# A decoder layer on one core: row sums of attention added on GpSimd, and the value products moved among the thirds of Q and K

## The reference, cut to what matters

```
qkv = x @ w_attn + b_attn ;  q, k, v = split(qkv), 16 heads of 32
att = softmax(where(causal, (q @ k.T) / sqrt(32), -inf))
y   = att @ v                      # per head
x   = layernorm(x + y @ w_proj + b_proj)
x   = layernorm(x + chosen(x))     # one of 4 experts by token id
x   = layernorm(x + routed(x))     # top 2 of 8 experts and a shared one
```

## Time and profile before

| what | value |
|---|---|
| median of 3 runs | 1278.62 us (1278.06 to 1281.37) |
| profiled execution, its own time | 1269.57 us |
| its span | 1267.7 us |
| mean granted PE clock | 0.968 |
| busy, share of span: PE, weight load, DVE, ACT, POOL | 93%, 74%, 54%, 36%, 19% |
| attention stage, roughly | 0 to 450 us of the span |

### The profile page before, as it was taken

How to read it: one execution, slowest core, us unless ns; L and a number is a source line. 1 busy time by engine, 2 the same in 40 slices (tenths; PEclk the granted TensorE clock), 3 DMA queues, 4 the chain that set the end, 5 groups by cost and what they waited for, 6 DMA issues and landing times.

```text
span 1267.7 us, 20196 instructions
## 1 busy us (share of the span) xinstructions
PE 1183.1 (93%) x6404; PEld 935.7 (74%) x6404; DVE 686.9 (54%) x1469; ACT 456.2 (36%) x699; POOL 240.8 (19%) x370
## 2 busy tenths in 40 slices
PE   7788999999999879994999999999999999999996
PEld 5565676576575558883688888899999997778885
DVE  5564656656557546664447634343444442666744
ACT  3254435334435322222343334244444433333331
POOL 2021314413414410003100440000000000433200
PEclk8989999999999979997999999999999999999998
DMA  7336573532524222225223666245345531666440
GB/s 241 86 100 238 179 249 118 133 88 51 150 61 125 80 85 83 84 76 157 101 82 93 208 227 199 79 149 175 122 145 172 171 99 53 206 178 195 144 139 33
DMA packets 129277, 169.72 MB, mean 134 GB/s; under 512 B 17553, under 2 KB 70801, under 8 KB 129169
## 3 DMA queue, kind: packets, MB, share of 16 engines
q1 hardware_dynamic: 115360, 136.64, 35.2%
q0 software_dynamic: 8496, 28.32, 6.7%
q10 hardware_dynamic: 5312, 3.42, 1.2%
HBM read 95.98 MB, written 47.19 MB: 113 GB/s over the span
## 4 chain that ended last, share of the span: by engine, by line
PE 74%; DVE 8%; SPq 5%; POOL 3%; DMA 3%; issue 3%; ACT 2%; ACTq 1%; POOLq 0%; DVEq 0%
PE routed_ps L819 18%; PE routed_ps L1370 16%; PE psT L471 11%; SPq L354 5%; PE chosen_psG L819 4%; PE chosen_psY L819 4%; PE routed_ps L1389 2%; PE routed_ps L1390 2%; PE routed_ps L1391 2%; PE psS L537 2%; PE psO L576 2%; POOL routed_rows_io L1308 2%; PE psN L576 2%; PE psE L558 2%; PE routed_ps L1411 1%
## 5 line engine op out<-in xcount | busy, mean ns | idle before, releaser
L471 PE MATMUL psT<-store 128*128 128x512 f32 x576 | 157.2, 408 | 5.4 <-DVE store L685 3.5
L754 DVE CUSTOM_DVE_ANT_0 psS<-psS,attn_mask 128x512 f32<-128x512 f32 (+3 forms) x256 | 120.8, 510 | 60.3 <-PE psS L537 60.3
L641 ACT ACTIVATE acc<-psE 128x512 f32<-128x512 f32 x160 | 93.7, 599 | 141.7 <-PE psE L558 138.2
L1370 PE MATMUL routed_ps<-routed_later,routed_held 128*128 128x512 f32 x528 | 127.3, 398 | 3.6 <-issue 2.9
L1370 PE MATMUL routed_ps<-routed_first,routed_held 128*128 128x512 f32 x528 | 128.0, 396 | 1.4 <-DVE routed_first L1809 1.4
L471 PEld LDWEIGHTS psT<-store 128*128 128x128 f32 x576 | 105.7, 195 | 25.1 <-issue 4.0
L1370 PEld LDWEIGHTS routed_ps<-routed_later,routed_held 128*128 128x128 f32 x528 | 100.5, 192 | 28.0 <-DVE routed_held L1713 3.5
L819 PE MATMUL routed_ps<-routed_held,routed_h_hi 128*128 x624 | 116.1, 328 | 0.5 <-DVE routed_h_lo L1754 0.3
L1370 PEld LDWEIGHTS routed_ps<-routed_first,routed_held 128*128 128x128 f32 x528 | 99.7, 191 | 22.2 <-DVE routed_first L1809 1.8
L1308 POOL DMA_INDIRECT routed_rows_io<-sorted_y,routed_pos x32 | 37.6, 1175 | 387.8 <-DMA sorted_y<-routed_rows_io 314.0
L413 POOL TENSOR_SCALAR_AFFINE_SELECT acc<-acc 128x256 f32<-128x256 f32 (+1 forms) x160 | 57.2, 365 | 274.0 <-ACT acc L641 273.7
(11 more groups left out here) (249 smaller groups left out, 1973.8 us busy)
## 6 DMA issues: line engine op xcount, KB each, us to landing
sorted_x<-attn_zero SPq DMA_DIRECT2D x19, 768.0 KB, 5.9
routed_sraw<-in_L_ffn_Sg_dram SPq DMA_DIRECT2D x44, 256.0 KB, 3.1
routed_sraw<-in_L_ffn_Su_dram SPq DMA_DIRECT2D x44, 256.0 KB, 3.5
routed_sraw<-in_L_ffn_Sd_dram SPq DMA_DIRECT2D x44, 256.0 KB, 4.0
routed_rows_io<-sorted_x SPq DMA_DIRECT2D x39, 256.0 KB, 3.0
sorted_y<-routed_rows_io SPq DMA_DIRECT2D x39, 256.0 KB, 2.3
attn_qS<-attn_ch_hi SPq DMA_DIRECT2D x128, 64.0 KB
attn_kS<-attn_ch_hi SPq DMA_DIRECT2D x112, 64.0 KB
```

The source lines that it names most:

```text
L471: last = pe.matmul(out, lhs[a](k), rhs[c](k), start=(s[-1] == 0 and k == 0), stop=(s[-1] == 2 and k == KC - 1))
L641: act.activation(p_f[:, u, :], psE[:, n % 2, :], ACT.Exp, scale=SCALE).then_inc(exp_done, 1)
L754: last = dve.tensor_tensor_reduce(scores, scores, mask[:, (3 - t) * P:T], 1.0, BELOW_ALL, ALU.add, ALU.max, rowmax[:, g % 2, t, i:i + 1])
L1370: last = pe.matmul(out, w[:, slot, at + k * P:at + (k + 1) * P], x_part(k), start=(g == 0 and k == 0), stop=(g == 2 and k == KC - 1))
```

## The change

For groups 0 to 12 (`in_sums`), the four key tiles of a head are added on POOL in place into `p_f[:, 0:4, :]` after their causal cut, in four adds (AD 0 and 1: key tile 1 of two heads each, 768 elements a partition; AD 2: key tile 3, 512; AD 3: key tile 2, 1024), and one product with ones over the sum (RS, 512 columns, four heads) takes the place of the ones products of the four tiles. The first add waits for the value product of key tile 0, since it writes over what that reads. In the list, PV 0 now stands before Q, the adds among the parts of Q, the other PV after the parts of K, then one P1 and RS; NORM follows after one more P1. The exponentials of the next group, unit 0, wait for RS and all PV. For such steps, LZ moves behind the last add. Groups 13 to 15 are as before.

```
+def in_sums(g, NG):
+    return g < NG - 3
...
+        summed = s and in_sums(s - 1, NG)
+        pieces = [("PV", s - 1, j) for j in order] if summed else []
+        if summed:
+            steps += pieces[:1]
         for n, one in enumerate(head):
             steps += [one] + left[n:n + 1] + (p1[n - 3:n - 2] if n >= 3 else [])
             if n == 3:
                 steps += [("M", s)]
+            if summed and n < 3:
+                steps += [("AD", s - 1, n)]
+            if summed and n >= 3:
+                steps += pieces[n - 2:n - 1]
+                if n == 3:
+                    steps += [("AD", s - 1, 3)]
+                    if at == 3 and b and b < B - 1:
+                        steps += [("LZ", b)]
...
-        if s:
+        if summed:
+            steps += p1[:1] + early[:1] + [("RS", s - 1)] + early[1:]
+            p1 = p1[1:]
+        elif s:
...
+                elif kind == "AD":
+                    g, part = s[1:]
+                    if part < 2:
+                        heads = slice(2 * part, 2 * part + 2)
+                        at, more_p = p_f[:, heads, P:T], p_f[:, 4 + 2 * part:6 + 2 * part, 0:3 * P]
+                        pool.wait_ge(pv_done, pv_before(g) + 1)
+                        pool.wait_ge(mask_done, UNITS * g + 6 + 2 * part)
+                    elif part == 2:
+                        at, more_p = p_f[:, 0:4, 3 * P:T], p_f[:, 4:8, 3 * P:T]
+                        pool.wait_ge(sum_done, 4 * g + 2)
+                    else:
+                        at, more_p = p_f[:, 0:4, 2 * P:T], p_f[:, 8:10, :].rearrange("p u (h n) -> p (u h) n", h=2)
+                        pool.wait_ge(mask_done, UNITS * (g + 1))
+                        pool.wait_ge(sum_done, 4 * g + 3)
+                    pool.tensor_tensor(at, at, more_p, ALU.add).then_inc(sum_done, 1)
...
-                    for to, values in ((psO, lambda i: v_f[:, j, (g % 4) * P + i * D:(g % 4) * P + (i + 1) * D]), (psN, lambda i: ones[:])):
+                    kinds = [(psO, lambda i: v_f[:, j, (g % 4) * P + i * D:(g % 4) * P + (i + 1) * D]), (psN, lambda i: ones[:])]
+                    for to, values in kinds[:1] if in_sums(g, NG) else kinds:
...
+                elif kind == "RS":
+                    g = s[1]
+                    pe.wait_ge(sum_done, 4 * (g + 1))
+                    for i in range(4):
+                        last = pe.matmul(psN[i * D:(i + 1) * D, :], ones[:], p_f[:, i, :], start=True, stop=True, tile_position=(0, i * D))
                     last.then_inc(pv_done, 1)
...
-                    if u in (0, 4, 8) and g:
-                        act.wait_ge(pv_done, QT * (g - 1) + {0: 1, 4: 3, 8: 4}[u])
+                    if g and in_sums(g - 1, NG):
+                        if u == 0:
+                            act.wait_ge(pv_done, pv_all(g - 1))
+                    elif u in (0, 4, 8) and g:
+                        act.wait_ge(pv_done, pv_before(g - 1) + {0: 1, 4: 3, 8: 4}[u])
```

More of the change, by code:

```diff
@@ L152, in attention_phase, with pv_before, pv_all @@
             hi_order[s[:-1] if s[0] in ("Q", "K") else s] = len(hi_order)
+    def pv_before(g):
+        return sum(QT + in_sums(n, NG) for n in range(g))
+    def pv_all(g):
+        return pv_before(g + 1)
     def first(s):
@@ L276, in attention_phase @@
         pv_done = sem("pv_done")
+        sum_done = sem("sum_done")
         flip_done = sem("flip_done")
@@ L577, in _ @@
                                              start=(j == 0), stop=(j == 2), tile_position=(0, i * D))
+                    last.then_inc(pv_done, 1)
+                elif kind == "RS":
[3 more added lines that the diff above has]
+                        last = pe.matmul(psN[i * D:(i + 1) * D, :], ones[:], p_f[:, i, :], start=True, stop=True, tile_position=(0, i * D))
                     last.then_inc(pv_done, 1)
@@ L759, in _ @@
                     if part == 0:
-                        dve.wait_ge(pv_done, QT * (g + 1))
+                        dve.wait_ge(pv_done, pv_all(g))
                         dve.transpose(flip, psN[:]).then_inc(flip_done, 1)
```

## The result

The changed kernel took 1317.8 us (median of four runs, 1316.8 to 1319.1) against 1278.3 us in the runs beside it: a ratio of 1.032, with a 95% interval from 1.027 to 1.036. It is slower by 39.5 us, twice the 20 us forecast. The direction was right, the time lies above the range.

A forecast was written before the change was run, and what follows sets the result against it. PE was taken to bound long attention steps, with SP's transfers near-limiting short ones. Step changes summed to +17.6 us, the clock added +2.2: about +20, so 1298.6 us for the median, range 1280 to 1314.

The forecast's parts named there:

- PE's saving: PE, groups 0 to 12: ones products shrink, 4.87 to 3.59 us, 1.28 less per group, 16.6 over 13.
- Adds: POOL: the four new adds take 7.3 us a group, bounds 5.8 and 9.5.
- POOL ready: Last add done 12.6 us into step 6 and 16.1 into step 7, behind PE by 2.3 and 4.9 us.
- The tail: Step end: six P1 units and NORM behind the ones product wait for DVE, some 6.6 us to the next step.
- rival (c): Slower still: POOL and DVE collide, adds take 9.5 us instead of 7.3, 1314 us; chance 0.08.
- (a): Faster: POOL's adds are hidden because scatters and residual adds finish 5 us earlier, 1272 us; chance 0.14.
- (b): Same: the tail costs nothing and the adds are cheap, 5.8 us, no clock term, 1278 us; chance 0.10.
- PE's clock, +2.2: After POOL waits PE's clock falls: 1.1 us charged in steps 8 and 12, none in 7 and 11; bounds 0 to 7.7.
- Steps 7 and 11: Short steps with POOL's scatters or residual work ahead of the adds: 23.7 us against 19.1, +4.6 each.
- Steps 1 to 3: First steps of attention: no change, because SP's stacking transfers pace them.
- Steps 4, 8 and 12: Long steps with V products covering DVE: 1.28 us saved, 4.9 us waiting for POOL, +2.0 each before clock.
- Steps 5 and 9: Long steps with the output projection: POOL ready before PE, no wait, so -1.28 us each.

The follow-up runs named there:

- order_only: Changed kernel's list order, but all four ones products back, no adds on POOL and no product over the sum: 1308.7 us, ratio 1.028.
- extra products: Changed kernel plus unread 512-column products where PE waits, ahead of the product over the sum and of late P1 units in short steps: 1298.2 us, ratio 1.019.
- POOL's bursts moved: Changed kernel with the four scatters and four residual adds moved behind the last of the adds in POOL's order: 1291.4 us, ratio 1.014.
- best1: Changed kernel, scatters and residual adds late, two P1 units earlier, first value product behind Q's first third, x transposes later: 1287.6 us, ratio 1.007.
- long_only: Sum on POOL only for groups 3, 4, 7, 8, 11, 12, in the better order; other steps as in the kernel before: 1264.7 us, ratio 0.992.

## Why the prediction was wrong

**What held.** The cost model of the queues. PE's saving is 1.28 us a group (7.7 for six; 7 to 9 measured). Adds: 7.3 us forecast, 7.46 measured in step 6. POOL ready, from the start of the step: forecast 12.6 and 16.1 in steps 6 and 7, measured 12.1 (221.67) and 16.3 (246.63). The Trainium skill, GPSIMD Engine Reference, gives about 2.6 cycles at 1.2 GHz for each element of a two-input add (section 3.1), by estimate 2.2 ns; the trace agrees, (2363 - 1279) / 512 = 2.1. The tail waits for DVE, as forecast, but takes 7.6 us in step 6 and 7.8 in step 7 instead of 6.6. Step 6 took 20.7 us (forecast 20.2). POOL and DVE did not collide: no add took over 2.39 us, so rival (c) is out. Rivals (a) and (b), the faster and the same, are out by the measured time.

**The step that failed: PE's clock, +2.2.** I priced one fall of 1.1 us in steps 8 and 12, took the long waits for POOL as its only cause, and said that nothing is lost in the short steps, "whose tail waits for DVE". The clock fell in every short step, and in the tail itself: in order_only, without any add, two waits of 0.56 and 1.57 us and sparse P1 and P2 between them came before the fall. In the changed kernel some 7 us of value product, Q and P2 then ran at half speed. The extra products measure the term at 15 to 20 us where I had 2.2; the whole gap between forecast and result is 19.5. The distances between M copies show where the forecast missed (us against the kernel before; the last column is what the extra products gave back):

| distances | forecast | measured | given back |
|---|---|---|---|
| 0 to 3 | 0 | +7.7 | 5.9 |
| 4, 8, 12 | +8.2, clock included | +15.9 | 2.0 |
| 5, 9, 13 | -3.8 | -0.4 | 0 |
| 6, 10 | +6.2 | +7.2 | 4.0 |
| 7, 11 | +9.2 | +11.5 | 1.3 |
| 14 | 0 | +1.8 | 1.7 |

So in 6, 7, 10 and 11 the sum came out nearly right: there the slow clock took the place of waits that I had counted for POOL. The clock explains most of the excess in the first row and little of that in the second.

I had the earlier trace rows in hand, took the fall in it for that of one long wait (there were two, of 2.15 and 1.07 us), and read only two thirds of it. The stretch behind shows the rest, 1.3 us more at the low level, which makes up to 1.7 us a fall and not 1.1:

```profile
120.00:124.00 4.00, 4.00 (x25) 2.16 (x23) 1.58 (x4) 2.01 (x2) 0.00 (x0) 0.84 0.98 368
```

The Trainium skill, TensorE: Matmul & The Clock Gate, "HAM oscillation", says that idle time in a loop lowers the clock anew on each round; the trace agrees, and the sentence that weighed it (5.5 us more) pointed the right way. But the page's example is one long wait a round, and I counted the two waits of 2.3 us on it as well. The falls here came behind shorter waits still, for DVE too, in steps 1 to 3 as well, and each cost more than 1.1 us of full-speed work.

**Steps 7 and 11, +4.6 forecast, +6.0 and +7.0 measured** (first PE instructions, 230.33 to 255.47 and 342.99 to 369.13, against 19.1). In step 7 POOL was ready when forecast, but PE only at 13.8 us instead of 11.2, since it had gone through the head at half speed; so the wait was 2.5 and not 4.9. The waits for POOL that the profile shows (15 us on PE) are thus smaller than my sum (29 us), and the clock has taken their place. With POOL's bursts moved, 21 to 26 us came back for 13 us less of waiting: the terms are not separate. In step 8 the granted clock goes to 0.59 (272 to 276 us) behind the wait of 2.65 us for the adds.

**Steps 1 to 3, 0 forecast, about +8 measured** in the four distances that hold them. I let SP pace them. They were 22.9, 26.9, 21.5 and 21.0 us against 21.1, 20.8, 21.7 and 20.9: SP does pace the last two, not the first two. In step 1, PE waited for x (1.70 and 1.13 us), whose transposes the new list puts together, and for maxima, and ran at 0.81. I had not followed the transposes; but with them moved (best1) the step stays at 27.0 us, so they are not all of it.

**Steps 4, 8 and 12, +2.0 forecast each, +4.9, +4.1 and +3.6 measured** between first PE instructions (step 8: 255.47 to 290.49, 35.0 us). They begin at half speed, with what the tail before them left behind. At their end, the next step's first value product, now ahead of Q, waits 0.88 us for DVE to add the bias to V, a wait that Q had covered; I named nothing behind that move. Placed behind the first third of Q (best1), it no longer waits.

**Steps 5 and 9, -1.3 forecast, +0.5 measured** (31.3 to 31.8). PE's busy time in them fell by 0.6 us and its idle time rose from 1.2 to 2.3: the waits for DVE's low half of the transposed x (1.15 us against 0.66), for ACT's exponentials (0.40) and for DVE (0.33) are new or longer. In long_only, with P1 moved forward as well, the same steps gain 1.5. Which of its edits does it is not shown.

## What to carry to other kernels

A clock fall need not come from one long wait: waits of 0.5 and 1.6 us with thin work between them were followed by some 7 us of work at half speed, in one round of the loop after the other. What that costs depends on what sets the pace: 64 us less at the low level were worth 15 to 20 us in one order, and 34 us less were worth 1 to 7 in another. Work that is moved to balance one engine has to leave something beside each serial stretch of the others; here six score units, the normalisation and all exponentials behind one product left a gap that the old order did not have. Before an idle engine is given work that others wait for, look at what stands ahead of it in its queue: moving five us of that back, in five steps, was worth 21 to 26 us, and applying the change only to steps with other work to cover it turned 3.2% slower into 0.8% faster.

## What the hardware showed that I had not expected

PE's clock fell to the 1.2 GHz level after a stretch in which PE was still busy for 1.75 of 4 us, with no wait over 1.6 us in it, and stayed there for about 6.8 of the next 8 us though PE then worked without a break. And 121 products that nobody reads made the kernel 15 to 20 us faster.
